# Batch-end normalization and query work placed elsewhere in the hand-written step order of a decoder kernel

## The reference

```python
x = x + _L0_attn_ref(_layernorm(x), ...)       # gated slot attention, 16 heads
x = x + _L0_xattn_ref(_layernorm(x), ctx, ...) # cross attention with projections
x = x + _L0_ffn_ref(_layernorm(x), ...)        # 8 experts, top 2
x = x + _L1_attn_ref(_layernorm(x), ...)       # differential attention, 16 heads ("da")
x = x + _L1_xattn_ref(_layernorm(x), ctx, ctx) # causal cross attention, no weights ("ca")
x = x + _L1_ffn_ref(_layernorm(x), ...)        # gated feed forward
```

## Time and profile before

| | us |
|---|---|
| median of 3 runs | 2006.92 |
| lowest and highest | 2005.13, 2010.65 |
| profiled execution, its own time | 2005.13 |
| its span, from the first to the last instruction | 2003.3 |
| TensorE busy (share of the span) | 1765.3 (88%) |
| VectorE busy | 1300.5 (65%) |
| ScalarE busy | 845.4 (42%) |
| GpSimd busy | 506.5 (25%) |
| granted TensorE clock, mean | 0.937 |

### The profile page before, as it was taken

The page is one execution under the profiler, slowest core; times in us unless marked ns, Lnnn a source line. Parts: engine busy times, 40 slices in busy tenths (PEclk is TensorE's granted clock), DMA queues, the critical chain, the costliest instruction groups (busy, mean ns, idle before and its releaser), DMA issues.

```text
span 2003.3 us, 32246 instructions
## 1 busy us (share of the span) xinstructions
PE 1765.3 (88%) x12150; PEld 1102.0 (55%) x12150; DVE 1300.5 (65%) x2924; ACT 845.4 (42%) x1363; POOL 506.5 (25%) x864
## 2 busy tenths in 40 slices
PE   5998999998966979979979979998888889999977
PEld 4898888888643334434334445664454444444446
DVE  6767676766576687686678642444345687888743
ACT  2343433333331345355446732442232356666651
POOL 5443444434121020120121113441111223331200
PEclk9999999999986999999999979998897899999988
DMA  3000100110016387236055046554603057656000
GB/s 116 22 12 11 43 11 12 34 53 1 16 41 123 60 174 94 56 82 92 33 104 70 2 160 232 182 195 105 133 1 53 24 71 144 81 91 83 6 1 22
DMA packets 91396, 142.65 MB, mean 71 GB/s; under 512 B 14549, under 2 KB 59737, under 8 KB 91242
## 3 DMA queue, kind: packets, MB, share of 16 engines
q1 hardware_dynamic: 86842, 127.72, 30.4%
q10 hardware_dynamic: 2528, 7.74, 1.1%
q0 software_dynamic: 1872, 5.13, 0.7%
HBM read 109.62 MB, written 32.03 MB: 71 GB/s over the span
## 4 chain that ended last, share of the span: by engine, by line
PE 64%; DVE 18%; issue 5%; DMA 5%; ACT 4%; SPq 2%; POOL 2%; another core or an unknown queue 0%; DVEq 0%; POOLq 0%; ACTq 0%
PE bank L1181 8%; PE bank L1221 8%; PE bank L1200 7%; PE bank L1913 5%; PE bank L1523 5%; PE bank L1804 3%; PE bank L766 3%; PE bank L1806 3%; PE bank L1805 3%; PE bank L1932 2%; DVE xa_part_max L1294 2%; PE bank L2373 2%; DMA xa_qst<-xa_q_parts 2%; PE bank L2358 2%; DMA xa_k_parts<-xa_parts 2%
## 5 line engine op out<-in xcount | busy, mean ns | idle before, releaser
L1294 DVE TENSOR_REDUCE xa_part_max<-bank 128x1 f32<-128x448 f32 (+1 forms) x512 | 270.4, 568 | 66.0 <-PE bank L1181 62.0
L1255 ACT ACTIVATE xa_e<-bank 128x1024 f32<-128x1024 f32 (+1 forms) x208 | 212.4, 1021 | 133.3 <-PE bank L1200 131.5
L1255 ACT ACTIVATE ca_e<-bank 128x1024 f32<-128x1024 f32 (+2 forms) x208 | 196.3, 956 | 92.5 <-PE bank L1200 91.5
L1294 DVE TENSOR_REDUCE shared<-bank 128x1 f32<-128x400 f32 (+1 forms) x384 | 206.8, 570 | 40.5 <-PE bank L1181 36.9
L1181 PE MATMUL bank<-xa_kst,xa_qst 122*128 122x448 bf16 (+1 forms) x512 | 167.6, 365 | 45.0 <-DVE xa_part_max L1294 18.5
L1221 PE MATMUL bank<-xa_e,xa_vaug 128*17 128x256 f32 (+2 forms) x1792 | 141.0, 389 | 1.6 <-ACT xa_e L1255 0.6
L1200 PE MATMUL bank<-xa_qst,xa_kst 128*128 128x256 bf16 (+1 forms) x832 | 129.6, 279 | 4.7 <-DMA xa_qst<-xa_negT 4.7
L1221 PE MATMUL bank<-ca_e,ca_vaug 128*17 128x256 f32 (+2 forms) x1664 | 125.6, 374 | 2.0 <-ACT ca_e L1255 1.4
L1181 PEld LDWEIGHTS bank<-xa_kst,xa_qst 122*128 122x128 bf16 x512 | 45.9, 99 | 147.8 <-DVE xa_part_max L1294 86.3
L1181 PE MATMUL bank<-ca_kst,ca_qst 125*128 125x400 bf16 (+2 forms) x384 | 118.3, 341 | 7.5 <-issue 3.5
L970 POOL TENSOR_TENSOR gsa_qk<-gsa_qk,gsa_rot 128x512 f32<-128x512 f32 x64 | 81.8, 1279 | 163.0 <-DVE gsa_rot L886 163.0
(11 more groups left out here) (382 smaller groups left out, 4095.7 us busy)
## 6 DMA issues: line engine op xcount, KB each, us to landing
xa_kst<-xa_k_parts SPq DMA_DIRECT2D x96, 200.1 KB, 8.4
ca_kst<-ca_k_parts SPq DMA_DIRECT2D x96, 200.1 KB, 7.9
xa_k_parts<-xa_parts SPq DMA_DIRECT2D x8, 1200.8 KB, 6.8
ca_k_parts<-moe_ctx_parts SPq DMA_DIRECT2D x8, 1200.8 KB
moe_gu<-in_expert_gate_up SPq DMA_DIRECT2D x8, 1024.0 KB
shared<-in_ctxT_split ACTq DMA_DIRECT2D x4, 1601.0 KB, 6.6
moe_ctxT<-in_ctxT SPq DMA_DIRECT2D x8, 800.5 KB, 8.1
ca_cv<-in_ctx SPq DMA_DIRECT2D x4, 1536.0 KB
```

What stands on the lines that cost most here:

```text
L1255: e.activation(self.e[m % 3][0:rows, :, first:T], banks[m % 2][0:rows].rearrange("p a (h t) -> p (a h) t", t=T)[:, :, first:T], ACT.Exp, s ...
L1294: e.tensor_reduce(top, work[:, 0:hi - lo], AX.X, ALU.max).then_inc(*reduced(t, *step))
```

## The change

Nothing is computed differently. Positions of steps change, and two helpers become one:

```diff
@@ flow (the fifth stage, after a batch's last unit; m is the tile after it)
-   yield from spread(steps[:-len(turns)], *((m + 8.3, m + 9) if self.masked else (m + 4, m + 8.7)))
+   yield from spread(steps[:-len(turns)], *((m + 7.6, m + 9) if self.masked else (m + 4, m + 8.7)))
@@ helpers
-def added(b, at, unit):
-
-    return [(at + p * unit, s) for p, s in ((0, ("out_turn", b, 0)), (0.1, ("out_turn", b, 1)), (0.6, ("out", b, 0)), (0.8, ("out", b, 1)))]
-
-def queries_of(b, at, unit):
+def finished(b, at, unit):
 
     norms = list(norm_steps(4, b))
-    return [(at + p * unit, s) for p, s in spread(norms[:-TB], 0, 0.3) + [(1.4, norms[-2]), (1.6, norms[-1]), (2, ("ca_q", b))]]
+    steps = [(0, ("out_turn", b, 0)), (0.1, ("out_turn", b, 1)), (0.6, ("out", b, 0)), (0.8, ("out", b, 1))]
+    steps += spread(norms[:-TB], 1.1, 1.4) + [(2.5, norms[-2]), (2.7, norms[-1]), (3.1, ("ca_q", b))]
+    return [(at + p * unit, s) for p, s in steps]
@@ da_steps (the fourth stage)
-   parts.append(added(n // UNITS, n + 3.2, 1))
-   if n + UNITS + 1 < N_DA:
-       parts.append(queries_of(n // UNITS, n + 4.3, 1))
+   parts.append(finished(n // UNITS, n + 3.2, 1 if n + 4 < N_DA - 1 else 0.75))
...
-(14.9, ("neg", 0)), (14.9, ("neg_parts", 0)), (15.6, ("neg_turn", 0))
+(14.9, ("neg", 0)), (15.1, ("neg_parts", 0)), (15.6, ("neg_turn", 0))
@@ ca_steps (the fifth stage)
-parts += [queries_of(B - 2, 0.4, 4.5), added(B - 1, 3.2, 5), queries_of(B - 1, unit + 8.4, 4.5)]
+parts.append(finished(B - 1, 3.2, 0.5 * unit))
```

More of the change, by code:

```diff
@@ L2306, in da_steps @@
                 if n % UNITS == UNITS - 1 and n + 1 < N_DA:
-                    parts.append(added(n // UNITS, n + 3.2, 1))
-                    if n + UNITS + 1 < N_DA:
-                        parts.append(queries_of(n // UNITS, n + 4.3, 1))
+                    parts.append(finished(n // UNITS, n + 3.2, 1 if n + 4 < N_DA - 1 else 0.75))
             first = [("max", 0, h_, i, c) for h_ in range(UNIT) for i in range(TB) for c in range(len(ca_chunks))]
-            parts.append([(9.7, ("load", 0)), *spread(first, 10.9, 14.9), (14.9, ("neg", 0)), (14.9, ("neg_parts", 0)), (15.6, ("neg_turn", 0))])
+            parts.append([(9.7, ("load", 0)), *spread(first, 10.9, 14.9), (14.9, ("neg", 0)), (15.1, ("neg_parts", 0)), (15.6, ("neg_turn", 0))])
             return merged(*parts)
```

## The result

| | before | changed |
|---|---|---|
| median of 4 runs each | 2006.03 us | 2028.15 us |
| lowest and highest | 1998.38, 2010.65 | 2023.70, 2032.28 |
| span of the profiled execution | 2003.3 | 2024.2 |
| its mean granted clock | 0.937 | 0.934 |

The ratio is 1.0105, 95% interval 1.0076 to 1.0136: slower by 15 to 27 us, where 2027 was forecast, +21.2. Busy times hardly moved; the time is in waits.

The account below looks back on a forecast made before the run. The chain of waits lay 64% on TensorE and 18% on VectorE, with hardly any TensorE slack in the fifth stage. The terms 10.6 - 0.3 + 10.9 gave +21.2 us, hence 2027 us, range 2014 to 2034.

Parts of the forecast that it names:

- (a): End of the fourth stage: batch 2's normalization and queries added there delay the fifth stage's start, +10.6 us, bounds 9 and 12.
- (b) and (c): Fifth stage's start: batch 2's groups gone, batch 3's `norm_stats` earlier, ahead of `neg_parts 1`; -0.3 us, bounds -4 and +2.5.
- c: Fifth stage's start: batch 3's `norm_stats` moves from 21.4 to 10.35, so `neg_parts 1` stands behind it on GpSimd.
- (d): Three places in the fifth stage: earlier adds and `norm_stats` put `neg_parts` behind the root; +10.9 us, bounds 5.4 and 13.
- the faster rival: Whole change: the root on GpSimd delays nobody; -7.3 us, 1998 on the profiled time; chance 0.07.
- The other two: Rivals: no measurable change, about +5 us, 2010, chance 0.08; slower only by (a), +13 us, 2018, chance 0.10.

Follow-up runs that it names:

- tail_parts_first: The changed kernel with `neg_parts 0` back at 14.9, ahead of `norm_stats` on GpSimd; ratio 1.0127 to the kernel before.
- no_d: The changed kernel with the fifth stage's adds and normalization back at 8.3 behind m instead of 7.6; ratio 1.0055 to the kernel before.
- turns_last: The changed kernel with `neg_parts 0` at 14.9 and batch 2's two `norm_turn` and `ca_q` behind fin 15; ratio 1.0124 to the kernel before.
- c_only: The kernel before with only batch 3's normalization and queries moved to 10.35 of the fifth stage; ratio 1.0034, and 1.0031 when run again.
- b2_later: d_parts_first with batch 2's normalization and queries at 21.4 of the fifth stage and batch 3's at 34.5; ratio 0.9981 to the kernel before.
- d_parts_first: d_only with `neg_parts` at hi + 0.3 instead of hi + 0.4 in the fifth stage, ahead of the root; ratio 0.9973 to the kernel before.
- d_only: The kernel before with only the fifth stage's adds and normalization behind a batch moved from 8.3 to 7.6 behind m; ratio 1.0069.
- root_short: d_only with one round of the inverse root on GpSimd instead of three in the fifth stage; ratio 1.0029 to the kernel before.

## Why the prediction was right

- **(a) The fourth stage's end: +10.6 forecast, +10.32 measured by the span's clock, +11.0 from exp 15's start.** The steps came as worked out: root 4.33 us (1565.89 to 1570.22), `neg_parts` behind the first `norm`, TensorE idle 5.91 us, pv 15 at half clock (1.91 us), 4.56 us from the cast to the end of the issues. All of it stands 0.9 us earlier than I had it, and the doubled pv took the 0.9 back. The 0.5 us that I credited to the early `out` steps isn't shown: the last add is 0.67 earlier, but 0.54 of that is there before the moved steps begin (L2375 at 1559.93, L2379 at 1560.47 before). The bound of 9 to 12 held. One reading would have misled: I named the late `neg_turn 0` the core of the forecast, and in this place it is worth 0.9 us of 11 (tail_parts_first); the sum was right because it followed the chain to the boundary.
- **(b) and (c): -0.3 forecast, -0.65 measured** at unit 4 (99.75 us against 100.40). That the two numbers lie so close is luck: the other three kernels with this start of the fifth stage came to +1.1 (no_d), +0.15 (tail_parts_first) and -1.2 (turns_last). The mechanism is shown. L1187 ahead of unit 1 waits 3.29 us for GpSimd; the step to unit 1, +0.7 forecast, was +1.1 (+0.8 to +2.4 in the other three); and the step from unit 2 to unit 3 gives 1.5 back, where I had 1.0. That batch 3's root eats what batch 2's removal gives is shown from both sides: c_only moves unit 1 by +3.1, b2_later by -2.2. What c did in the sixth stage when alone was not in my reasons and is not explained.
- **(d): +10.9 forecast, +12.1 measured** (S +11.46, less -0.65 at unit 4). `neg_turn` is 3.44 us later in each of the three batches, 3.5 forecast. By batch it is 3.2, 4.0 and 4.9 us, where I had 3.4, 3.4 and 4.1. The low clock followed all three stalls, which was the choice between 5.4 and 10.9. The rule that I had weighed, that waits between bursts send the clock to half speed (the Trainium skill, "TensorE: Matmul & The Clock Gate", section "HAM oscillation — how this bites in real kernels"), agrees with the three rows of 0.56 to 0.60. One price was worked out wrongly: 7 us times 0.24 is 1.7 us for the lost clock of a batch and not 1.9. With 1.7 the lower bound of (d) is 5.8 and the faster rival's gain in (d) 7.3.
- The marks add up to +21.8, the sixth stage took 0.9 us less, and the span grew by 20.9. That the forecast of +21.2 lies so near is partly luck: (a) counted from exp 15 and (d) were 0.4 and 1.2 us more than forecast, and what ran ahead of exp 15 and the sixth stage, which were not in the sum, took 0.7 and 0.9 back.
- **The rivals.** The faster one named what decides it: if the root delays nobody, (d) gives -7.8. d_parts_first is that case, and gave 5.3 us: the clock came back in full (1.00 three times), VectorE's waits went, but of the 1.06 us that TensorE waited for a `norm` in batch 2 it still waits 0.62. The other two fall with d_only and no_d: neither half alone is the whole.

## What to carry to other kernels

In a list of steps that every engine walks in order, moving a step moves its parts in all the queues: look in each queue for the short operation that others wait for and that the moved long one now overtakes. Here 14 tiny dependent operations ahead of 4 tiny ones stopped three engines, and the early adds that cost 12 us gain 5 with the two swapped. Ahead of a boundary count the whole chain of what is added, not the first step that is late: it costs all by which it reaches past the work that was already there.

## What the runs showed of the hardware

A stall of TensorE costs more than its length: in batch 2, where the clock had stayed full before, `neg_turn` is 3.44 us later, and from there to the last exp it takes another 1.4 us (59.1 against 57.7), though the wait of 1.06 us for a `norm` in that stretch is gone. How the clock answered to the wait ahead of L1187, over 7 us from it, in the three batches: no wait, 1.00, 1.00, 1.00 (d_parts_first); 1.6 us, 0.76, 0.76, 1.00 (before); 1.8 us, 0.56, 0.76, 0.76 (root_short); 4.1 us, 0.72, 0.66, 0.63 (d_only) and 0.68, 0.63, 0.61 (changed). So waits of 1.6 us were followed by the low clock in two places and not in the third.

Small work on GpSimd hardly gets cheaper with fewer values: an operation on 128x2 values takes 0.19 to 0.23 us and one on 128x8 also 0.19 to 0.21, while one on 128x256 takes 1.22 (L369). Dependent ones follow each other every 0.27 to 0.31.

The kernel with batch 3's normalization alone moved took 6.5 us more in the sixth stage in both of its profiled executions, at a granted clock of 0.80 instead of 0.94 behind the stage's first 29.6 us; no row between explains it, and whether the order is the cause is not shown.
